# A fused attention and feed-forward kernel: x and q's factors brought into channel order by transposing transfers

## The chip, the cores and the metric

The kernel runs on one core of one Trainium2 chip. The metric is the device time of one launch in microseconds, as the median of three runs. A core has a matrix engine (TensorE, PE), a vector engine (VectorE, DVE), an activation engine (ScalarE, ACT), a general engine (GpSimd, POOL) and a queue engine (SyncE, SP) that here issues transfers; each goes through its own list of instructions in order, and they wait for each other through semaphores. 16 DMA engines do the transfers. SBUF is the on-chip memory of 128 partitions, PSUM the memory that TensorE writes.

## The reference, cut to what matters

```python
xn = layernorm(x)                                  # x: 2 x 2048 tokens x 256 channels
# attention on xn: a second layernorm with gain and bias, then
z = layernorm(xn) * g + b
q, _, v = split(z @ w_in.T + b_in); k = q          # 16 heads of 16 channels
out = softmax(q @ k.T / 4) @ v ; attn = out @ w_out.T + b_out
# feed-forward on xn, with weights rounded to -1, 0, 1
h = gelu(xn @ ternary(W1).T + b1); ffn = h @ ternary(W2).T + b2
return x + attn + ffn
```

The second normalisation of an already normalised token is one number per token, the factor. So q = (the product of xn with the scaled weights) times the factor of the token, plus a bias.

## The kernel before, in words

The 4096 tokens go through the first stage in 8 groups of 512 (NG = 8), each as 4 tiles of 128 tokens. After it comes the attention over 32 pairs of batch and head, paced by VectorE's row maxima (line 889), and the output projection. The change touches only the first stage, some 200 of 1397 us.

TensorE contracts over partitions, so it needs x with channels on partitions ("channel order"), while the normalisation makes it with tokens on partitions ("token order"). Before, this goes as follows in group g:

- VectorE in `stats_of(g + 1)` and `norm(g + 1)`: means and variances of the next group (L754 to L764), a power on GpSimd (`rsqrt`, L657), then `xn` in token order (L772) and the factor columns (L777). GpSimd spreads the factor over 128 columns (`replicate`, L662).
- TensorE at the start of its `group(g)`: 8 transpositions of `xn` (L1170) and 4 of the factor replicas (L1154), all float32 128x128, into the PSUM banks `tr_x` and `tr_f`.
- ScalarE copies `tr_x` scaled to float16 (`x1`, L1038) and `tr_f` to `factor_rows` (L1031). VectorE makes the remainder, `x2 = tr_x * 256 - x1` (`second_parts`, L784). x1 + x2 carries x nearly in float32 precision through float16 products.
- TensorE then: the second half of the values of group g - 1 (`values(g-1, 1)`, L1135), the down projection of g - 1 (`ffn_down`, L1115, 64 products), the q products of g (L1135, 12), the up projection (L1198, 8 columns of weights f = 0 to 7, two PSUM banks in turn, so that f waits for the GELU of f - 2), with the first half of the values after f = 3.
- From group 2 on, TensorE puts steps of the first head's row maxima between (`between`, L359, 4 in a group), which VectorE reduces (`first_rows`, L889).
- VectorE in a group: `second_parts(g)`, `stats_of(g+1)`, `value(g-1, 1)` (L802), `norm(g+1)`, `add_ffn(g-1)` twice (L810), `q_split(g)` (L791 twice, L795 twice), and `results(g)`: 4 remainders of the hidden layer (L881) with row maxima between. ScalarE: the first part of q (L1059) as soon as L791 has made it, then GELU twice (L1063) and the first part of the hidden layer (L1068), four times.
- SyncE: `store_q(g)` (L545, 2 transfers). After group 1 and after group 3 it waits for the stores and loads pieces of the first heads (8, then 24 transfers, L553 to L556), in the same queue.

The order is written out by hand in each engine's program. In the attention SyncE uses one small transposing transfer in each head (L564, 128x128 float16).

## Time and profile before

| | us |
|---|---|
| median of 3 runs (lowest, highest) | 1397.49 (1397.26, 1397.63) |
| the profiled execution: its own time | 1398.74 |
| its span, first to last instruction | 1397.0 |
| TensorE busy | 1367.5 (98%) |
| VectorE busy | 1328.5 (95%) |
| ScalarE busy | 1236.8 (89%) |
| GpSimd busy | 141.4 (10%) |

The mean granted TensorE clock is 0.994 of full speed. The shares are means over stages with different limits: what a change of the first stage is worth is read from that stage.

### The profile page before, as it was taken

Reading aid. Unit: us, or ns where it says so; the run is one execution under the profiler, and the core shown is the slowest. Engines: PE = TensorE matmul, PEld = TensorE weight load, DVE = VectorE, ACT = ScalarE, POOL = GpSimd, SP = SyncE. Lnnn points to the kernel's source line nnn. Section 1 sums busy time; section 2 is a strip of 40 time slices with the busy share of each in tenths; the row PEclk is TensorE's granted clock in tenths of the full one; section 3 lists DMA queues with packets and bytes.
Section 4 is the critical chain, followed back from the end, with each engine's and each line's share of the span. In section 5 each row is a group of like instructions: output and inputs, shape, how many; then the busy total and the mean of one; then the engine's idle time right before and its main releaser. Section 6 shows DMA issues by size and latency. Waiting matters only on the chain.

```text
span 1397.0 us, 32162 instructions
## 1 busy us (share of the span) xinstructions
PE 1367.5 (98%) x13350; PEld 467.5 (33%) x13350; DVE 1328.5 (95%) x1396; ACT 1236.8 (89%) x2244; POOL 141.4 (10%) x351
## 2 busy tenths in 40 slices
PE   6999999999999999999999999999999999999999
PEld 4656643222222222222222222222222222222244
DVE  6898999999999999999999999999999999999935
ACT  5564638999999999999999999899999999999975
POOL 2101034000000000000000000000222200002200
PEclk8999999999999999999999999999999999999999
DMA  6112000011110001001001001001122201012122
GB/s 239 27 38 65 31 18 2 33 32 33 33 33 33 32 33 33 33 33 33 33 33 33 32 31 35 26 28 39 51 64 60 63 32 34 33 35 63 40 89 98
DMA packets 33916, 61.75 MB, mean 44 GB/s; under 512 B 11392, under 2 KB 16928, under 8 KB 33514
## 3 DMA queue, kind: packets, MB, share of 16 engines
q1 hardware_dynamic: 33194, 58.04, 12.5%
q8 instruction: 105, 1.72, 0.5%
q10 hardware_dynamic: 576, 1.65, 0.3%
q14 instruction: 41, 0.34, 0.1%
HBM read 41.29 MB, written 16.77 MB: 42 GB/s over the span
## 4 chain that ended last, share of the span: by engine, by line
DVE 70%; PE 25%; issue 2%; DMA 1%; ACT 1%; POOL 0%; ACTq 0%; SPq 0%; DVEq 0%; POOLq 0%
DVE part_max L889 68%; PE ps L389 6%; PE ps L403 3%; PE ps L1198 3%; PE ps L359 3%; PE ps L1115 3%; PE ps L1135 2%; PE ps L480 2%; PE ps L461 1%; DMA rows<-in_rows 1%; ACT w L1092 1%; PE ps L450 1%; PE ps L490 0%; PE ps L1170 0%; DMA max_rows<-max_split 0%
## 5 line engine op out<-in xcount | busy, mean ns | idle before, releaser
L1092 ACT ACTIVATE w<-ps 128x512 f32<-128x512 f32 x2048 | 1109.5, 596 | 65.9 <-PE ps L403 16.5
L889 DVE TENSOR_REDUCE part_max<-ps 128x1 f32<-128x1024 f32 x1024 | 1161.1, 1212 | 4.1 <-PE ps L359 3.8
L389 PE MATMUL ps<-w,v_ones 128*32 128x256 f32 (+1 forms) x7688 | 627.8, 398 | 0.6 <-DVE resid L810 0.3
L403 PE MATMUL ps<-qry,key 50*128 50x512 f16 x1984 | 399.0, 387 | 7.7 <-ACT w L1092 6.9
L359 PE MATMUL ps<-qry,key 48*128 48x512 f16 x2048 | 393.9, 381 | 5.3 <-DVE part_max L889 5.3
L389 PEld LDWEIGHTS ps<-w,v_ones 128*32 128x32 f32 x7688 | 151.5, 108 | 313.2 <-issue 160.7
L403 PEld LDWEIGHTS ps<-qry,key 50*128 50x128 f16 x1984 | 98.1, 92 | 430.2 <-ACT w L1092 412.1
L359 PEld LDWEIGHTS ps<-qry,key 48*128 48x128 f16 x2048 | 99.9, 93 | 82.6 <-DVE part_max L889 16.6
L681 POOL COPY v_ones<-v_all 128x128 f32<-128x128 f32 x64 | 18.7, 293 | 748.8 <-PE ps L389 748.8
L1059 ACT ACTIVATE q_split<-q_by_factor,sigma_bq 128x512 f16<-128x512 f32 x16 | 11.1, 719 | 63.0 <-DVE q_by_factor L791 62.6
L1198 PE MATMUL ps<-x,w_ternary 128*128 128x512 f16 x256 | 62.4, 382 | 1.6 <-ACT hidden L1063 1.6
L1115 PE MATMUL ps<-w_ternary,w 128*128 128x256 f16 x448 | 51.3, 273 | 0.2 <-DVE w L881 0.2
L1063 ACT ACTIVATE hidden<-ps,columns 128x512 f32<-128x512 f32 x64 | 41.8, 678 | 6.6 <-PE ps L1198 5.6
L1115 PEld LDWEIGHTS ps<-w_ternary,w 128*128 128x128 f16 x448 | 43.3, 98 | 6.7 <-issue 1.4
L955 DVE SCALAR_TENSOR_TENSOR resid<-ps,y_unscale,resid 128x512 f32<-128x512 f32 x16 | 12.0, 750 | 33.1 <-PE ps L480 33.1
L881 DVE SCALAR_TENSOR_TENSOR w<-hidden,hidden_scale,w 128x1024 f16<-128x1024 f32 x28 | 35.7, 1281 | 6.5 <-ACT w L1068 6.5
L688 POOL TENSOR_TENSOR max_rise<-part_max 128x16 f32<-128x16 f32 x32 | 7.9, 248 | 274.4 <-DVE part_max L889 274.4
L1198 PEld LDWEIGHTS ps<-x,w_ternary 128*128 128x128 f16 x256 | 22.6, 98 | 32.9 <-issue 6.8
L1068 ACT ACTIVATE w<-hidden,hidden_scale 128x1024 f16<-128x1024 f32 x28 | 32.2, 1149 | 1.0
L1135 PE MATMUL ps<-x,wq_parts 128*128 128x512 f16 x96 | 24.6, 410 | 3.7 <-ACT factor_rows L1031 3.7
L657 POOL TENSOR_TENSOR rstd<-var_eps,minus_half 128x8 f32<-128x8 f32 x8 | 13.5, 1690 | 118.5 <-DVE var_eps L764 118.5
L1135 PE MATMUL ps<-wv_parts,x 128*128 128x256 f16 x192 | 23.6, 273 | 0.0
(151 smaller groups left out, 481.1 us busy)
## 6 DMA issues: line engine op xcount, KB each, us to landing
key<-q_parts SPq DMA_DIRECT2D x62, 128.0 KB
qry<-q_parts SPq DMA_DIRECT2D x62, 128.0 KB
o_heads<-o_evacuated SPq DMA_DIRECT2D x31, 256.0 KB, 9.8
key<-q_parts SPq DMA_DIRECT2D x66, 64.0 KB
qry<-q_parts SPq DMA_DIRECT2D x66, 64.0 KB
resid<-in_x SPq DMA_DIRECT2D x8, 512.0 KB, 13.7
q_parts<-q_split SPq DMA_DIRECT2D x16, 256.0 KB, 2.3
out<-resid SPq DMA_DIRECT2D x7, 512.0 KB, 4.7
```

Of the source, the lines that this page charges most:

```text
L359: mm = eng.matmul(pair[:, j * BANK:(j + 1) * BANK], key[v][r:r + ROWS, blk * P:(blk + 1) * P], qry[v][r:r + ROWS, c * BANK:(c + 1) * BANK] ...
L389: mm = eng.matmul(pv[32 * c:32 * c + 2 * D, c0:c1], vst[:, kb, :], prob[kb % 2][:, c * BANK + c0:c * BANK + c1], start=(kb == 0), stop=(kb ...
L403: eng.matmul(ring_bank(v, i, False), key[v][r:r + KROWS, kb * P:(kb + 1) * P], qry[v][r:r + KROWS, c * BANK:(c + 1) * BANK], start=True, s ...
L480: mm = eng.matmul(py[:, j * C:(j + 1) * C], o_parts(g, k)[0:rows, a, t * P:(t + 1) * P], wop[0:rows, b, k, :], start=(m == 0), stop=(m == ...
L881: dve.scalar_tensor_tensor(out=part[1], in0=hid[:, 2 * i:2 * i + 2, :], scalar=hs[:, 0:1], in1=part[0], op0=ALU.mult, op1=ALU.subtract).th ...
L889: dve.tensor_reduce(part_max[h % 2][:, blk, side:side + 1], pa[a % 2], AX.X, ALU.max).then_inc(s_r, 1)
L1063: act.activation(hid[:, f, :], pf[f % 2], ACT.Gelu, scale=1.0 / XS, bias=b1_col[:, f:f + 1]).then_inc(s_g, 1)
L1068: act.activation(parts_of(g)[0][:, f - 1:f + 1, :], hid[:, f - 1:f + 1, :], ACT.Identity, scale=hs[:, 0:1]).then_inc(s_h1, 1)
L1092: act.activation(prob[kb % 2][:, c * BANK:(c + 1) * BANK], ring_bank(k, i, last), ACT.Exp, scale=exp_scale).then_inc(s_e, 1)
L1115: mm = pe.matmul(pf[t // 2][:, (t % 2) * C:(t % 2 + 1) * C], parts_of(g)[i][:, f, t * P:(t + 1) * P], w2t[:, f, :], start=(f == 0 and i == ...
L1135: mm = pe.matmul(out, rows(k, i, j), cols(k, i, j), start=(m == 0), stop=(m == len(terms) - 1))
L1198: mm = pe.matmul(pf[f % 2], w1t[:, k, f * P:(f + 1) * P], part[:, k, :], start=(k == 0 and i == 0), stop=(k == KC - 1 and i == 1))
```

## The change

For groups 1 to 7 the float16 parts of x are made in token order and both are transposed by one transfer; the same for the factors, split into two float16 parts by GpSimd. Group 0 stays on TensorE. The float32 factor is scaled by 2^14 before it is split, and the products with `factor_rows` take 2^-14 back.

- ScalarE: `stage_first(g+1)` makes 256 * `xn` in float16, 128x1024, in place of L1038 twice and L1031. It stands ahead of q's first part.
- VectorE: `stage_second(g+1)` makes the remainder, 128x1024, and stands between `add_ffn` and `q_split`; `second_parts` ahead of `stats_of` goes.
- GpSimd: `replicate` makes two float16 parts of the replicas (a small scaling, a cast, a subtraction of 128x512); `factor_rows(g)` adds the two transposed parts (128x512).
- SyncE: `x_parts_in(g+1)` ahead of `store_q(g)`: a transfer of 8 blocks of 128x128 for the factors and one of 16 blocks for x.
- TensorE: from group 1 on no transpositions; q waits for `s_xt`, the x transfer.

```diff
+        xt = [sb(f"x_parts{i}", [P, 2, KC, BANK], F16) for i in range(2)]
+        xs = scr[:, 2:4, :].rearrange("p i n -> p (i n)").bitcast(F16).rearrange("p (s n) -> p s n", s=2)
...
+            def x_parts_in(g):
+                sp.wait_ge(s_fb, 3 * g + 1)
+                wait(sp, s_fr, g)
+                sp.dma_start_transpose(f_parts[:, :, :].rearrange("p s (t n) -> p (s t) n", n=P),
+                                       f_rep_parts[:, :, :, :].rearrange("p s t n -> p (s t n)")).then_inc(s_fx, 16)
+                sp.wait_ge(s_xs, g)
+                wait(sp, s_v, 2 * (g - 1))
+                sp.dma_start_transpose(xt[g % 2][:, :, :, :].rearrange("p s k (t n) -> p (s k t) n", n=P),
+                                       xs[:, :, :].rearrange("p s n -> p (s n)")).then_inc(s_xt, 16)
...
-            for g in range(HALF_GROUPS):
+            def group(g):
+                if g + 1 < NG:
+                    x_parts_in(g + 1)
                 store_q(g)
...
             def replicate(g):
                 pool.wait_ge(s_fc, 2 * (g + 1))
-                wait(pool, s_ft, g)
-                pool.tensor_copy(f_rep[:, :, :], f_col[:, g % 2, :].unsqueeze(2).to_broadcast((P, TG, P))).then_inc(s_fp, 1)
+                pool.tensor_tensor(f_big[:, :], f_col[:, g % 2, :], f_times[:, :], ALU.mult).then_inc(s_fb, 1)
...
+                pool.tensor_copy(f_rep_parts[:, 0, :, :], big).then_inc(s_fb, 1)
+                pool.wait_ge(s_fb, 3 * g)
+                pool.tensor_tensor(f_rep_parts[:, 1, :, :], big, f_rep_parts[:, 0, :, :], ALU.subtract).then_inc(s_fb, 1)
+
+            def factor_rows(g):
+                pool.wait_ge(s_fx, 16 * g)
+                pool.wait_ge(s_qf, KC * g)
+                pool.tensor_tensor(f_row[:, :], f_parts[:, 0, :], f_parts[:, 1, :], ALU.add).then_inc(s_fr, 1)
...
+            def stage_second(g):
+                dve.wait_ge(s_xa, g)
+                wait(dve, s_xt, 16 * (g - 1))
+                dve.scalar_tensor_tensor(out=xs[:, 1, :], in0=xn[:, :, :].rearrange("p a b -> p (a b)"), scalar=XS, in1=xs[:, 0, :],
+                                         op0=ALU.mult, op1=ALU.subtract).then_inc(s_xs, 1)
...
             for g in range(1, NG - 1):
-                second_parts(g)
+                if g == 1:
+                    stage_second(1)
                 stats_of(g + 1)
...
                     add_ffn(g - 1, j)
+                stage_second(g + 1)
                 q_split(g)
...
+            def stage_first(g):
+                act.wait_ge(s_ln, 4 * g + 4)
+                wait(act, s_xt, 16 * (g - 1))
+                act.activation(xs[:, 0, :], xn[:, :, :].rearrange("p a b -> p (a b)"), ACT.Copy, scale=XS).then_inc(s_xa, 1)
...
                 wait(pe, s_vd, 2 * g)
-                pe.wait_ge(s_x2, KC * (g + 1))
-                pe.wait_ge(s_fr, g + 1)
+                if first:
+                    pe.wait_ge(s_x2, KC)
+                    pe.wait_ge(s_fr, 1)
+                else:
+                    pe.wait_ge(s_xt, 16 * g)
```

How the change moves instructions, at three places. First VectorE from the last hidden remainder of one group to the q products of the next, before:

```order
L881 SCALAR_TENSOR_TENSOR w<-hidden,hidden_scale,w 128x1024
L784 SCALAR_TENSOR_TENSOR x<-ps,x 128x512 x2
L754 BN_STATS stats<-resid 128x6 x4
L757 MEMSET wait_carrier 128x1
L759 BN_AGGR mean_var<-stats 128x2 x4
L763 TENSOR_SCALAR var_eps<-mean_var 128x4
L764 TENSOR_SCALAR var_eps<-mean_var 128x4
L802 SCALAR_TENSOR_TENSOR v_all<-ps,factor_columns,scaled_bv 128x256 x2
L770 TENSOR_TENSOR root_of_var<-var_eps,rstd 128x4
L772 TENSOR_SCALAR xn<-resid,mean_var,rstd 128x256 x4
L810 SCALAR_TENSOR_TENSOR resid<-ps,hidden_unscale,resid 128x512 x2
L791 TENSOR_TENSOR q_by_factor<-ps,factor_rows 128x512 x2
```

and now (`weight_scratch` is the tensor in which the staged parts `xs` lie):

```order
L936 SCALAR_TENSOR_TENSOR w<-hidden,hidden_scale,w 128x1024
L799 BN_STATS stats<-resid 128x6 x4
L804 BN_AGGR mean_var<-stats 128x2 x4
L808 TENSOR_SCALAR var_eps<-mean_var 128x4
L809 TENSOR_SCALAR var_eps<-mean_var 128x4
L857 SCALAR_TENSOR_TENSOR v_all<-ps,factor_columns,scaled_bv 128x256 x2
L815 TENSOR_TENSOR root_of_var<-var_eps,rstd 128x4
L817 TENSOR_SCALAR xn<-resid,mean_var,rstd 128x2x128 x4
L865 SCALAR_TENSOR_TENSOR resid<-ps,hidden_unscale,resid 128x512 x2
L838 SCALAR_TENSOR_TENSOR weight_scratch<-xn,weight_scratch 128x1024
L845 SCALAR_TENSOR_TENSOR q_by_factor<-ps,factor_rows 128x512 x2
```

The x remainder moved from the start of this stretch, for group g, to its end, for group g + 1, directly ahead of the q products.

TensorE at the boundary of two groups, before:

```order
L1198 MATMUL ps<-x,w_ternary 128x512 x8
L1170 MATMUL ps<-ident_f,xn 128x128 x8
L1154 MATMUL ps<-ident_f,factor_replicas 128x128 x4
L1135 MATMUL ps<-wv_parts,x 128x256 x12
L1115 MATMUL ps<-w_ternary,w 128x256 x64
L1135 MATMUL ps<-x,wq_parts 128x512 x12
```

and now:

```order
L1258 MATMUL ps<-x_parts,w_ternary 128x512 x8
L1196 MATMUL ps<-wv_parts,x_parts 128x256 x12
L1176 MATMUL ps<-w_ternary,w 128x256 x64
L1196 MATMUL ps<-x_parts,wq_parts 128x512 x12
```

The twelve transpositions are gone, and nothing else moved on TensorE.

SyncE's queue from the q store of group 0, before:

```order
L545 DMA q_parts<-q_split 128x2x512 x4
L553 DMA key<-q_parts 32x1x1024
L554 DMA key<-q_parts 16x1024
L555 DMA qry<-q_parts 32x1x1024
L556 DMA qry<-q_parts 16x1024
```

and now:

```order
L557 DMA q_parts<-q_split 128x2x512 x2
L563 DMA_TRANSPOSE factor_parts<-factor_replicas 128x8x128
L567 DMA_TRANSPOSE x_parts<-weight_scratch 128x16x128
L563 DMA_TRANSPOSE factor_parts<-factor_replicas 128x8x128
L567 DMA_TRANSPOSE x_parts<-weight_scratch 128x16x128
L557 DMA q_parts<-q_split 128x2x512 x2
L575 DMA key<-q_parts 32x1x1024
```

Two transposing transfers stand ahead of each q store and, through it, ahead of the loads of the first heads.

## Rows read from the trace of the kernel before

**Rows 1.** The page, part 4: the chain that ended last, by engine and by line.
```profile
DVE 70%; PE 25%; issue 2%; DMA 1%; ACT 1%; POOL 0%; ACTq 0%; SPq 0%; DVEq 0%; POOLq 0%
DVE part_max L889 68%; PE ps L389 6%; PE ps L403 3%; PE ps L1198 3%; PE ps L359 3%; PE ps L1115 3%; PE ps L1135 2%; PE ps L480 2%; PE ps L461 1%; DMA rows<-in_rows 1%; ACT w L1092 1%; PE ps L450 1%; PE ps L490 0%; PE ps L1170 0%; DMA max_rows<-max_split 0%
```

**Rows 2.** The chain in order of time, groups 2 and 3: start us, us, what.
```profile
73.33 0.32 PE ps L359 x2
...
82.39 0.87 PE ps L1170 x8
83.27 0.44 PE ps L1154 x4
...
97.07 1.83 PE ps L1198 x8
...
104.52 0.87 PE ps L1170 x8
```

**Rows 3.** Busy time in group 3: stretch, length, each engine (instructions), clock, DMA share, GB/s.
```profile
82.39:104.52 22.13, 22.13 (x155) 14.30 (x153) 20.00 (x38) 12.57 (x18) 2.25 (x2) 1.00 0.11 36
```

**Rows 4.** Timeline of group 3: start, us, engine, line, operation [idle before <-releaser].
```profile
84.51 1.28 DVE L881 SCALAR_TENSOR_TENSOR w<-hidden,hidden_scale,w 128x1024 f16<-128x1024 f32 x1 [0.26 <-ACT w L1068]
...
85.84 1.29 DVE L784 SCALAR_TENSOR_TENSOR x<-ps,x 128x512 f16<-128x512 f32 x2
...
89.22 1.64 POOL L657 TENSOR_TENSOR rstd<-var_eps,minus_half 128x8 f32<-128x8 f32 x1 [17.98 <-DVE var_eps L764]
90.95 0.16 DVE L770 TENSOR_TENSOR root_of_var<-var_eps,rstd 128x4 f32<-128x4 f32 x1 [1.04 <-POOL rstd L657]
...
92.40 1.40 DVE L810 SCALAR_TENSOR_TENSOR resid<-ps,hidden_unscale,resid 128x512 f32<-128x512 f32 x2
...
93.72 0.68 DVE L791 TENSOR_TENSOR q_by_factor<-ps,factor_rows 128x512 f32<-128x512 f32 x1
```

**Rows 5.** Timeline of group 1.
```profile
42.88 1.28 DVE L784 SCALAR_TENSOR_TENSOR x<-ps,x 128x512 f16<-128x512 f32 x2
43.02 4.26 PEld L1115 LDWEIGHTS ps<-w_ternary,w 128*128 128x128 f16 x40 [0.45 <-DVE w L881]
...
47.40 2.75 PE L1135 MATMUL ps<-x,wq_parts 128*128 128x512 f16 x12
...
50.76 1.27 DVE L791 TENSOR_TENSOR q_by_factor<-ps,factor_rows 128x512 f32<-128x512 f32 x2
...
53.51 1.90 PE L1198 MATMUL ps<-x,w_ternary 128*128 128x512 f16 x8 [1.38 <-ACT hidden L1063]
...
60.67 0.41 SPq L556 DMA_DIRECT2D qry<-q_parts  x1
```

**Rows 6.** Timeline of group 7, the first row maxima.
```profile
177.82 4.62 DVE L889 TENSOR_REDUCE part_max<-ps 128x1 f32<-128x1024 f32 x4 [1.40 <-PE ps L359]
```

**Rows 7.** The small transposing transfer, line 564: issue min/median/max in ns, then landing.
```profile
L564 SPq DMA_TRANSPOSE max_rows<-max_split x32: 1119/1132/1216, 202.3 to 1331.8; - x32
...
DMA to landing us min/median/max: 2.2/2.2/4.3
```

**Rows 8.** What the DMA engines moved, 40 slices of 203.0 to 204.4 us.
```profile
GB/s 0 0 0 0 0 0 0 0 0 0 0 0 0 0 0 73 95 183 219 190 117 51 7 0 234 0 0 0 0 0 0 0 0 1 0 1 1 0 0 0
```

**Rows 9.** The page, part 5: ScalarE's 128x1024 copies (busy us, mean ns | idle).
```profile
L1068 ACT ACTIVATE w<-hidden,hidden_scale 128x1024 f16<-128x1024 f32 x28 | 32.2, 1149 | 1.0
```

**Rows 10.** GpSimd's nearest operations: min/median/max ns, first and last start.
```profile
L714 POOL TENSOR_TENSOR x<-below_half,x x2: 1158/1160/1161, 1276.2 to 1279.3; 128x512 f16<-128x512 f32 x2
...
L688 POOL TENSOR_TENSOR max_rise<-part_max x32: 217/217/1183, 198.8 to 1330.3; 128x16 f32<-128x16 f32 x32
```

**Rows 11.** Granted clock around TensorE's idle time in group 0 (columns as in rows 3).
```profile
13.00:14.00 1.00, 0.34 (x4) 0.10 (x1) 0.00 (x0) 0.00 (x0) 0.00 (x0) 1.00 1.01 383
...
15.00:16.00 1.00, 0.00 (x0) 0.00 (x0) 0.56 (x2) 1.00 (x3) 0.37 (x1) 0.50 1.00 410
...
28.50:29.00 0.50, 0.50 (x4) 0.26 (x3) 0.49 (x1) 0.50 (x1) 0.50 (x1) 0.99 0.00 0
```

More of the change, by code:

```diff
@@ L32 @@
 HTOP = 2.0 ** 14
+FS = 2.0 ** 14
 AHEAD = 2
@@ L205, in attention_ffn @@
         r_rest = [f32(t, n)[0:HR, :] for t in (w1t, w2t) for n in range(2)]
-        on = [hid[:, n, :].bitcast(F16).rearrange("p (s n) -> p s n", s=2) for n in range(NT0)] + [x1, x2] + on_k
+        on = [hid[:, n, :].bitcast(F16).rearrange("p (s n) -> p s n", s=2) for n in range(NT0)] + [xt[0][:, s, :, :] for s in range(2)] + on_k
         on_rest = [scr[0:HR, n, :].bitcast(F16).rearrange("p (s n) -> p s n", s=2) for n in range(NCH)]
@@ L265, in attention_ffn @@
         s_x2 = sem("x2")
+        s_xa = sem("x_part1_staged")
+        s_xs = sem("x_part2_staged")
+        s_xt = sem("x_parts_transposed")
         s_fc = sem("factor_columns")
@@ L574, in _ @@
             sp.wait_ge(s_pad, 16 * (2 * ROT - 1))
-            for g in range(HALF_GROUPS):
+            def group(g):
+                if g + 1 < NG:
+                    x_parts_in(g + 1)
                 store_q(g)
+            store_q(0)
+            x_parts_in(1)
+            for g in range(1, HALF_GROUPS):
+                group(g)
             sp.wait_ge(s_qs, 16 * KC * HALF_GROUPS)
@@ L579, in _ @@
             for g in range(HALF_GROUPS, NG // NB):
-                store_q(g)
+                group(g)
             sp.wait_ge(s_qs, 16 * KC * NG // NB)
@@ L585, in _ @@
             for g in range(NG // NB, NG):
-                store_q(g)
+                group(g)
             sp.wait_ge(s_qs, 16 * KC * NG)
@@ L767, in norm @@
                 x = resid[:, g * TG:(g + 1) * TG, :]
-                wait(dve, s_tr, g)
+                wait(dve, s_tr, min(g, 1))
                 dve.wait_ge(s_rs, g + 1)
@@ L1071, in _ @@
             group(0, True)
+            act.wait_ge(s_wvp, 1)
+            stage_first(1)
             for g in range(1, NG):
@@ L1136, in part_products, with parts_x @@
                 return mm
-            xp = (x1, x2)
+            def parts_x(g):
+                return [xt[g % 2][:, i, :, :] for i in range(2)]
             def values(g, j):
@@ L1150, in factor_transposes @@
             def factor_transposes(g):
-                pe.wait_ge(s_fp, g + 1)
-                wait(pe, s_fr, g)
+                pe.wait_ge(s_fp, 1)
                 for t in range(TG):
@@ L1155, in factor_transposes @@
                 mm.then_inc(s_ft, 1)
-            def step_count(g):
-                return len(BETWEEN) * (min(max(0, g - HALF_GROUPS), HALF_GROUPS) + max(0, g - NG // NB))
             def group(g, between=None, between_down=None):
-                pe.wait_ge(s_ln, 4 * g + 4)
-                wait(pe, s_x2, KC * g)
-                if g == 1:
+                first = g == 0
+                xp = parts_x(g)
+                if first:
+                    pe.wait_ge(s_ln, 4)
+                    for k in range(KC):
+                        for t in range(TG):
+                            mm = pe.transpose(tr_x[k][:, t * P:(t + 1) * P], xn_kt[:, k, t, :], idf[:, :])
+                    mm.then_inc(s_tr, 1)
+                    abs_total(0)
+                    factor_transposes(0)
+                if g == HALF_GROUPS:
                     pe.wait_ge(s_wd, 5)
                     pe.wait_ge(s_od, 1)
-                wait(pe, s_r, step_count(g))
-                for k in range(KC):
-                    for t in range(TG):
-                        mm = pe.transpose(tr_x[k][:, t * P:(t + 1) * P], xn[:, t, k * P:(k + 1) * P], idf[:, :])
-                mm.then_inc(s_tr, 1)
-                first = g == 0
-                if first:
-                    abs_total(0)
-                factor_transposes(g)
                 if first:
@@ L1182, in group @@
                 wait(pe, s_vd, 2 * g)
-                pe.wait_ge(s_x2, KC * (g + 1))
-                pe.wait_ge(s_fr, g + 1)
+                if first:
+                    pe.wait_ge(s_x2, KC)
+                    pe.wait_ge(s_fr, 1)
+                else:
+                    pe.wait_ge(s_xt, 16 * g)
                 for o in range(KC):
```

67 lines of the change are left out of this document (40 added, 27 removed).

## The prediction

> **What bounds the kernel now.** I read the chain of waits first. Over the whole kernel it is VectorE with 70%, nearly all of it row maxima [rows 1]: from about 178 us on the kernel runs at VectorE's pace, and what reaches that point earlier ends earlier by as much. Before that point the same chain in order of time lies on TensorE: in group 3 it enters the transpositions of x at 82.39 and those of the factors at 83.27, leaves them at 83.70 (83.27 + 0.44), and is back at the same place at 104.52 [rows 2]. A group takes 22.13 us, of which 1.31 are transpositions. The busy time by stretch shows what stands close behind: VectorE is busy for 20.00 of these 22.13 us [rows 3], and 1.04 of the rest is its wait for GpSimd's power at 90.95 [rows 4], which no edit touches. So VectorE needs 21.04 us a group as it stands, TensorE without transpositions 22.13 - 1.31 = 20.82. TensorE cannot get all of its 1.31 us; the question is where VectorE and ScalarE stop it.
>
> **The loop that is left in groups 2 to 6.** The x remainder costs VectorE the same in either place: 1.29 us for its two PSUM halves [rows 4], and 1.28 for one 128x1024 from SBUF, by the hidden remainder of that form [rows 4]. The scaled q products are of the form of L784, which takes 0.68 like L791, so they cost nothing more. But the remainder moves from the start of VectorE's stretch, where TensorE had time, to directly ahead of the q products. Follow one turn:
>
> - from TensorE's last up product to the end of the last hidden remainder: 82.39 to 84.51 + 1.28 = 85.79, 3.40 us through two GELUs and a copy on ScalarE. Unchanged, as it hangs on TensorE's end.
> - from there to the start of the q products: 93.72 - 85.79 = 7.93 us, with L784 in it before, with the staged remainder after. VectorE is busy or waits for GpSimd's power throughout, so these 7.93 stay. ScalarE's part fits: L810 starts at 92.40, so xn is done by then, the copy takes 1.15 [rows 9], the two L810 take 1.32 to the next row.
> - from the q products' start to TensorE's f = 2, which needs the first GELU, which stands behind q's first part on ScalarE: 2.75 us, as group 1 shows, where TensorE waited for it: 50.76 to 53.51 [rows 5].
> - from f = 2 to the group's end on TensorE: 104.52 - 97.07 = 7.45 us [rows 2].
>
> Sum: 3.40 + 7.93 + 2.75 + 7.45 = 21.53 us a turn, against TensorE's own 20.82. Before, TensorE needed 22.13 and this loop had 0.6 us to spare; now the loop decides, and TensorE waits 0.71 us ahead of f = 2. **A group gains 22.13 - 21.53 = 0.6 us, not 1.31.** Five groups (2 to 6): -3.0 us.
>
> **Group 7.** VectorE sits idle for 1.40 us until TensorE's first step at 177.8 [rows 6]. The step stands behind the transpositions, so here all 1.31 us are gained; with the end of the idle time VectorE's row maxima begin, and the gain is carried to the end. -1.31 us.
>
> **Group 1.** Its transpositions cover nothing: TensorE waited right after them for VectorE's last hidden remainder until 43.02, with 40 down products left [rows 5]. So the q products can again start at 47.40 at the earliest, and now they need the x transfer. VectorE ends the staged remainder where L784 ended, at 42.88 + 1.28 = 44.16, and SyncE, with the factors' transfer long behind it, issues 16 blocks. The trace has a transfer of one block only: 1.13 us of issue and 2.2 to landing [rows 7], its data in 8 slices of 35 ns, 0.28 us, at 219 GB/s at the most [rows 8]. That leaves about 0.8 us after the data. Bounds for 16 blocks (512 KB): at 219 GB/s 1.1 + 2.4 + 0.8 = 4.3 us; with the 0.28 of a block 16 times 1.1 + 4.5 + 0.8 = 6.4; with the whole issue time of a block 16 times 18 + 1.1 = 19 us. I take 6.0, near the second, as the one block's data came in one burst and not spread over its issue. x then lands at 50.2. ScalarE may write the parts of group 2 only then: 1.15 us, VectorE 1.28, and the q products start at 52.7 instead of 50.76 [rows 5] (up to 5.4 us it would be 52.04, since the remainder follows L810 anyway). TensorE's f = 2 follows 2.75 us later, as before: +1.9 us.
>
> The Trainium skill prices such a transfer in two ways. "Advanced Engine Details and Errata", section X-Bar Transpose (TRN2), expects 350 to 400 GB/s, by which the data would take an estimated 1.4 us and the landing stay under 5.4 us; its rate isn't seen in the one block of this trace, 219 at the peak. "VectorE: DVE Perf Modes", section The three transpose paths, gives 1309 ns for a 128x128 block, near the issue of 1.13 here; if that holds for every block of a large transfer, the second rival below is what happens.
>
> **What else is added, and what hides it.** GpSimd makes the parts and adds them up, three operations of up to 1.16 us [rows 10] and a small one, about 3 us in a group in which it was busy for 2.25 [rows 3]; the rows are needed a group later. SyncE's 24 blocks stand ahead of the q store: at 0.28 a block plus two fixed costs some 9 of 21.5 us. The store lands later by as much, which ScalarE asks for only in the next group, and the loads of the first head after it (8 behind group 1, 24 behind group 3), whose first use is a step of the following group, had 12 us: the last of the 8 was issued by 61.1 [rows 5], the first step ran at 73.33 [rows 2]. The 24 behind group 3 take, at 0.41 or somewhat more each, 10 to 14 us and end about when the factors' parts of group 5 are ready. Nothing on the chain at that price. Losing this cover starts when SyncE's work exceeds a group.
>
> **Sum.** +1.9 - 3.0 - 1.31 = -2.4 us: 1396.3 against the profiled execution's 1398.74, and 1397.49 - 2.4 = **1395.1** against the median of the runs, which lies 1.25 below that execution. Its own range, from the bounds of the landing (4.3 gives +1.3, about 8 gives +3.9) and 0.3 us either way in each of five turns: 1393 to 1398.5.
>
> **Rivals.**
> 1. TensorE stays the bound, the loop closes faster than I add up. For it: TensorE is busy in all of the 22.13 us, and VectorE has 2.13 spare by the sum of its busy time. Against it: the order of the four links. It would give -6 x 1.31 + 1.3 = -6.6, 1390.9. Chance 0.12.
> 2. Transposing transfers cost per block. For it: the issue of one block takes 1.13 us, where that of a plain load of the first head takes 0.41 [rows 5]. Against it: the short burst [rows 8]. It turns the sign from where the x transfer lands 8.4 us after its issue (2.4 more than 6.0), so from 0.4 us a block. At 0.6 a block the landing takes 11.5 us and the sum is +3, 1400.6, with SyncE at 15 of 21.5 us and the 24 loads ahead of group 5's parts about to add some; at 1.13 a block SyncE alone needs 28 us a group, q of group 7 starts some 60 us late, and the time is near 1460. Chance 0.20, most of it in the lower half.
> 3. GpSimd's new work slows VectorE, with which it runs side by side: the subtraction falls on the staged remainder, which reads two SBUF tensors. For it: GpSimd's L688 took 1183 ns once instead of 217 [rows 10], so something can hold it up. Against it: no row here shows VectorE held up. If 1.16 us are lost in the loop in five groups, -2.4 + 5.8 = +3.4, 1400.9; from 0.5 us a group it is slower. Chance 0.08.
> 4. TensorE's clock falls in group 1. In group 0 TensorE went idle at 13.34, and the granted clock was 0.50 (1.2 GHz) by 15; it was back at 2.4 GHz from 28.5, 6 us after TensorE had resumed [rows 11]. The new wait ahead of q is 50.2 - 47.4 = 2.8 us; an idle time of 1.38 in this group brought no fall [rows 5]. Six us of products at half speed lose 3 us, partly beside the q products' own wait: +2, so 1397.1, within no change. Chance 0.15.
>
> **How the numbers follow.** The forecast has 0.45. A measurement of this kernel tells no change from 0.2%, 2.8 us either way: 1394.7 to 1400.3. The forecast lies within it by 0.4 us, so a third of its chance goes to faster (0.15), with rival 1 (0.12) that makes 0.27. Slower are rival 2 except its mild third (0.14), rival 3 in half its sizes (0.05) and 0.05 for rivals 3 and 4 or 2 and 4 together: 0.24. The rest, 0.49, is no change. The range reaches to 1390 for rival 1 and to 1403 for the mild half of rivals 2 and 3.
>
> **What would show it.** In the profile after: TensorE idle for some 0.7 us ahead of an up projection (f = 2) in groups 2 to 6, released by a GELU, and turns of 21.5 us; q products of VectorE right behind the staged remainder; TensorE idle for 2 to 3 us ahead of q in group 1, released by the x transfer; that transfer's landing near 6 us and SyncE's issue of it near 5; the first row maxima of group 7 near 175.4. Turns of 20.8 speak for rival 1; an issue of x near 10 or 18 us for rival 2; VectorE's 128x1024 remainder longer than 1.28 for rival 3; a clock of 0.5 near 50 us for rival 4. The forecast is wrong if the turns are under 21.2 or over 21.9, or if group 1 costs over 4 us.

## The result, and the profile after

| | before | after |
|---|---|---|
| median, us (lowest, highest; runs) | 1397.64 (1397.26, 1397.99; 6) | 1403.70 (1402.01, 1407.72; 6) |
| ratio to before, 95% interval | | 1.0044 (1.0035 to 1.0054) |
| profiled execution, its span | 1398.74, 1397.0 | 1403.02, 1401.2 |

Slower by 6.1 us, where 2.4 less were forecast, and outside the range (1403.0). The two profiled executions, from which all rows below are, lie 4.3 us apart: that of the kernel before is 1.1 us above its median, that of the kernel after 0.7 below. First the busy time of one turn, the stretch from one start of VectorE's q products to the next, which answers to [rows 3]. Columns: the stretch, its length, busy time of PE, PEld, DVE, ACT, POOL with their instructions, PE's granted clock, DMA share, GB/s.

```profile
97.34:119.47 22.13, 20.88 (x142) 12.97 (x140) 20.27 (x37) 11.82 (x15) 5.19 (x5) 1.00 0.47 111
```

TensorE's work did shrink to 20.88 us, and the turn is still 22.13, as before. VectorE's way to the q products, in order of time (start, duration, engine, line), answers to [rows 4]:

```profile
92.73 0.17 DVE L815 TENSOR_TENSOR root_of_var<-var_eps,rstd 128x4 f32<-128x4 f32 x1 [1.06 <-POOL rstd L685]
94.18 1.40 DVE L865 SCALAR_TENSOR_TENSOR resid<-ps,hidden_unscale,resid 128x512 f32<-128x512 f32 x2
95.50 1.92 DVE L838 SCALAR_TENSOR_TENSOR weight_scratch<-xn,weight_scratch 128x1024 f16<-128x1024 f32 x1
97.34 1.27 DVE L845 SCALAR_TENSOR_TENSOR q_by_factor<-ps,factor_rows 128x512 f32<-128x512 f32 x2
```

GpSimd at the same time:

```profile
94.61 0.61 POOL L699 CAST factor_replicas<-factor_scaled 128x512 f16<-128x512 f32 x1
95.30 1.04 POOL L701 TENSOR_TENSOR factor_replicas<-factor_scaled,factor_replicas 128x512 f16<-128x512 f32 x1
```

And all seven staged remainders (minimum, median, maximum in ns):

```profile
L838 DVE SCALAR_TENSOR_TENSOR weight_scratch<-xn,weight_scratch x7: 1211/1918/1922, 43.9 to 164.3; 128x1024 f16<-128x1024 f32 x7
```

The remainder that was priced at 1.28 takes 1.92 wherever GpSimd's subtraction had begun 0.20 us before it, and 1.21 the one time (43.9) that GpSimd was idle. TensorE waits behind it for the GELU, for 1.42 us at 77.97 and 1.25 at 168.94.

TensorE in group 1, answering to [rows 5], and the two transfers:

```profile
43.99 4.54 PE L1176 MATMUL ps<-w_ternary,w 128*128 128x256 f16 x40 [0.93 <-DVE w L936]
49.50 2.75 PE L1196 MATMUL ps<-x_parts,wq_parts 128*128 128x512 f16 x12 [0.98 <-DMA x_parts<-weight_scratch]
56.27 1.90 PE L1258 MATMUL ps<-x_parts,w_ternary 128*128 128x512 f16 x8 [2.28 <-ACT hidden L1122]
```

```profile
L567 SPq DMA_TRANSPOSE x_parts<-weight_scratch x7: 1771/2026/4330, 45.1 to 166.5; - x7
DMA to landing us min/median/max: 4.3/4.4/8.0
L563 SPq DMA_TRANSPOSE factor_parts<-factor_replicas x7: 1232/1239/9487, 34.1 to 165.2; - x7
DMA to landing us min/median/max: 3.2/3.3/14.2
```

f = 2 comes at 56.27 instead of 53.51: +2.8 us, although x lands sooner than was taken, 4.4 us after its issue. The maxima (4330 ns of issue, 9487 ns, 14.2 us) are one place, SyncE's queue behind group 3:

```profile
103.50 0.63 SPq L575 DMA_DIRECT2D key<-q_parts  x1
...
117.63 2.37 SPq L577 DMA_DIRECT2D qry<-q_parts  x1
120.05 2.14 SPq L578 DMA_DIRECT2D qry<-q_parts  x1
122.30 9.49 SPq L563 DMA_TRANSPOSE factor_parts<-factor_replicas  x1
131.88 4.33 SPq L567 DMA_TRANSPOSE x_parts<-weight_scratch  x1
```

and what hangs on it, on GpSimd and then on VectorE:

```profile
136.59 1.15 POOL L706 TENSOR_TENSOR factor_rows<-factor_parts 128x512 f32<-128x512 f16 x1 [18.12 <-DMA factor_parts<-factor_replicas]
137.70 1.65 POOL L685 TENSOR_TENSOR rstd<-var_eps,minus_half 128x8 f32<-128x8 f32 x1
```

```profile
139.45 0.16 DVE L815 TENSOR_TENSOR root_of_var<-var_eps,rstd 128x4 f32<-128x4 f32 x1 [3.51 <-POOL rstd L685]
```

GpSimd adds the rows of group 5 before it makes the power of group 6, in program order; the rows' parts land at 136.5, so VectorE's wait for the power is 3.51 us instead of 1.06. In group 7 TensorE's first products for row maxima begin at 181.63; the first row maximum, which answers to [rows 6], is at 182.07 instead of 177.82, +4.2 us, and that difference stays to the end (span 1401.2 against 1397.0).

### The profile page after: what moved, and what is told of

It reads as the page before. It is cut to its first block, busy times and chain, and to the rows that moved or that the text cites. A ratio compares the mean times of both kernels' runs of the same rounds, so it can differ in the third digit from the quotient of the medians.

```text
span 1401.2 us, 32007 instructions
## 1 busy us (share of the span) xinstructions
PE 1357.5 (97%) x13266; PEld 456.4 (33%) x13266; DVE 1333.4 (95%) x1389; ACT 1232.2 (88%) x2230; POOL 161.5 (12%) x374
## 4 chain that ended last, share of the span: by engine, by line
DVE 79%; PE 12%; DMA 3%; ACT 2%; issue 2%; SPq 1%; POOL 1%; ACTq 0%; DVEq 0%
DVE part_max L944 73%; PE ps L401 3%; PE ps L492 2%; PE ps L415 2%; PE ps L1258 1%; PE ps L371 1%; PE ps L473 1%; DMA factor_parts<-factor_replicas 1%; DMA rows<-in_rows 1%; DVE weight_scratch L838 1%; DVE w L936 1%; ACT hidden L1122 1%; PE ps L462 1%; DMA max_rows<-max_split 1%; POOL rstd L685 1%
## 5 line engine op out<-in xcount | busy, mean ns | idle before, releaser
L1258 PE MATMUL ps<-x_parts,w_ternary 128*128 128x512 f16 x256 | 61.9, 380 | 10.1 <-ACT hidden L1122 10.1
L1091 ACT ACTIVATE weight_scratch<-xn 128x1024 f16<-128x1024 f32 x7 | 7.4, 1054 | 45.0 <-DVE xn L817 45.0
L1258 PEld LDWEIGHTS ps<-x_parts,w_ternary 128*128 128x128 f16 x256 | 22.4, 98 | 41.0 <-ACT hidden L1122 14.2
L1196 PE MATMUL ps<-x_parts,wq_parts 128*128 128x512 f16 x96 | 23.5, 397 | 6.6 <-ACT factor_rows L1086 3.7
L1196 PE MATMUL ps<-wv_parts,x_parts 128*128 128x256 f16 x192 | 23.6, 273 | 0.0
```

The costliest lines, as they stand in the source:

```text
L1196: mm = pe.matmul(out, rows(k, i, j), cols(k, i, j), start=(m == 0), stop=(m == len(terms) - 1))
L1258: mm = pe.matmul(pf[f % 2], w1t[:, k, f * P:(f + 1) * P], part[:, k, :], start=(k == 0 and i == 0), stop=(k == KC - 1 and i == 1))
```

## The experiments

All are told by one ruler: the start of VectorE's q products in groups 1 to 7 (L791 before, L845 after), from the trace of each. Turns are the differences. Each ratio is to the kernel before in the same session (its medians there were 1397.6 to 1398.2), so ratios compare better than medians.

| kernel | starts, us | turns | median, ratio (95%) |
|---|---|---|---|
| before | 50.8 71.8 93.7 115.9 138.0 160.1 185.9 | 21.0 21.9 22.1 22.1 22.1 25.8 | |
| after | 53.5 75.2 97.3 119.5 144.1 166.2 190.2 | 21.7 22.1 22.1 **24.6** 22.1 24.0 | 1403.70, 1.0044 |
| e1_spread | 53.8 77.1 99.2 121.3 143.5 165.6 189.6 | 23.3 22.1 22.1 22.1 22.1 24.0 | 1402.07, 1.0028 (1.0017 to 1.0040) |
| e2_onepart | 52.1 73.1 94.5 115.9 139.4 162.1 186.1 | 21.0 21.4 21.4 23.6 22.7 24.0 | 1399.08, 1.0004 (0.9995 to 1.0013) |
| e3_order | 52.3 72.1 93.0 113.8 142.9 164.3 188.8 | 19.9 20.9 20.9 **29.1** 21.4 24.5 | 1400.65, 1.0023 (1.0014 to 1.0032) |
| e4_xonly | 51.4 72.3 93.8 115.2 138.2 159.8 184.3 | 21.0 21.4 21.4 23.0 21.6 24.4 | 1396.89, 0.9990 (0.9981 to 0.9999) |
| e5_order_spread | 51.9 71.7 92.6 113.5 134.3 155.2 179.5 | 19.9 20.9 20.9 20.9 20.9 24.3 | 1392.32, 0.9962 (0.9949 to 0.9976) |
| e6_xonly_order_spread | 49.7 69.7 91.4 113.3 135.3 157.2 183.1 | 19.9 21.7 21.9 21.9 21.9 25.9 | 1396.23, 0.9987 (0.9978 to 0.9996) |
| e9_late_subtraction | 52.8 73.8 95.2 116.6 144.8 166.2 190.2 | 21.0 21.4 21.4 **28.2** 21.4 24.0 | 1402.88, 1.0042 (1.0028 to 1.0055) |
| e10_start | 50.3 70.1 91.0 111.9 132.8 153.6 177.9 | 19.9 20.9 20.9 20.9 20.9 24.3 | 1390.94, 0.9954 (0.9941 to 0.9968) |
| e11_late_spread | 53.0 74.0 95.5 116.9 138.3 159.7 183.7 | 21.0 21.4 21.4 21.4 21.4 24.0 | 1396.91, 0.9993 (0.9984 to 1.0002) |
| e12_late_spread_start | 51.2 72.2 93.6 115.0 136.4 157.9 181.9 | 21.0 21.4 21.4 21.4 21.4 24.0 | 1395.42, 0.9983 (0.9974 to 0.9992) |

**e1_spread: the queue alone.**

```diff
             load_columns(0, 0, L // 2, L // 2, s_ld[0])
-            for h in range(1, ROT):
-                load_head(h, h)
             for g in range(NG // NB, NG):
                 group(g)
+                if g - NG // NB + 1 < ROT:
+                    load_head(g - NG // NB + 1, g - NG // NB + 1)
```

> The 16 loads of heads 1 and 2 are issued 8 by 8 behind groups 4 and 5 instead of all behind group 3, so the transfers of the parts of group 5 no longer stand behind 24 loads. Queue theory: the factors' transfer of group 5 lands in 3 to 5 us instead of 14.2, VectorE's wait for GpSimd's power in group 5 falls from 3.51 to 1.06 us, 2.5 us less in all (near 1401), and the runs lie closer together. Rival (GpSimd against VectorE explains all of the loss): no change beyond 0.5 us.

The long turn is gone (22.12), the staged remainder still takes 1.92. The profiled execution lost 1.6 us of its gain in an earlier turn (23.3 for 21.7): TensorE waited 2.30 us ahead of f = 2 in group 1, and its products behind that, and a stretch within them, read

```profile
56.52 3.54 PE L1258 MATMUL ps<-x_parts,w_ternary 128*128 128x512 f16 x8 [2.30 <-ACT hidden L1122]
...
57.00:59.00 2.00, 2.00 (x6) 0.68 (x5) 0.74 (x1) 1.74 (x3) 0.82 (x1) 0.50 1.09 298
```

a granted clock of 0.50 (1.2 GHz) where the kernel after has 1.00 (2.4 GHz) with an idle time of 2.28 at the same place, and 1.90 us for the same 8 products. That is what the fourth rival described. In the trace the gain of the turn is plain, 2.5 us; in the times it is 1.6 us, smaller than expected, with an interval that overlaps that of the kernel after. The seven executions do lie closer together, as expected: 1401.4 to 1402.8, against 1402.0 to 1407.7.

**e2_onepart: GpSimd's two-input operations out.** The second part of the factors is set to zero and the rows are a copy of the first: the factors have float16 precision only.

```diff
-                pool.tensor_tensor(f_rep_parts[:, 1, :, :], big, f_rep_parts[:, 0, :, :], ALU.subtract).then_inc(s_fb, 1)
+                pool.memset(f_rep_parts[:, 1, :, :], 0.0).then_inc(s_fb, 1)
...
-                pool.tensor_tensor(f_row[:, :], f_parts[:, 0, :], f_parts[:, 1, :], ALU.add).then_inc(s_fr, 1)
+                pool.tensor_copy(f_row[:, :], f_parts[:, 0, :]).then_inc(s_fr, 1)
```

> Leaves out the second float16 part of the factors of groups 1 to 7: GpSimd fills it with zeros instead of subtracting, and copies the first part instead of adding two. The transfers stay. Contention theory (VectorE's operations on two SBUF tensors are held up while GpSimd runs one with two inputs): the staged remainder takes 1.21 us in all seven groups instead of 1.92 in six, the stretched remainders near 33 and 37 us go back to 2.35 and 1.28, and the time falls by 0.95 + 6 x 0.71 = 5.2 us, to about 1398.5. Rival (the remainder is slow by its own form or because of the transfers): it stays at 1.92 and the time within 1 us.

```profile
L838 DVE SCALAR_TENSOR_TENSOR weight_scratch<-xn,weight_scratch x7: 1208/1215/1219, 43.1 to 161.0; 128x1024 f16<-128x1024 f32 x7
```

The remainder is back at 1.21 in all seven, although GpSimd's memset, which reads nothing, still lies beside its first 0.29 us (93.33 to 93.62), and two turns are 21.41 us: the forecast's loop of 21.53. The turn of 23.6 is the queue's. The one of 22.7 behind it begins with q products of TensorE at a granted clock of 0.50 (4.44 us for the 12 of 2.75), after 2.16 us of idle time, for which VectorE waits 0.97. The time fell by 4.6 us, near the expected 5.2.

**e3_order: the remainder behind the q products.** `q_split(g)` stands ahead of `stage_second(g + 1)`, nothing else changes.

> The staged remainder stands behind q_split instead of ahead of it. Loop theory (the place of the remainder ahead of the q products makes TensorE wait for the first GELU): TensorE's wait of 1.25 to 1.4 us at f = 2 goes, and a turn falls from 22.13 to what VectorE needs, 21.1 to 21.6: 5 x 0.5 to 1.0, time 1399 to 1401.5. The subtraction of GpSimd now falls on operations that read PSUM, so the remainder may take 1.21 as well. Rival (VectorE's sum of work decides, not the order): turns stay near 22.1, no change.

Turns of 20.87 us, TensorE's own time. But then one of 29.1: most of what was gained by group 4 is lost in the queue, whose end hardly moves (SyncE, factor parts and x parts of group 5; compare 122.30 and 131.88 in the kernel after):

```profile
121.60 9.34 SPq L563 DMA_TRANSPOSE factor_parts<-factor_replicas  x1
131.04 5.52 SPq L567 DMA_TRANSPOSE x_parts<-weight_scratch  x1
```

The loads begin at 102.82, where they began at 103.50, although group 3 is 4.4 us ahead: the x transfer of group 4 now waits for a later remainder (97.18), and the q store and the loads stand behind it. The long wait has a second price. TensorE is idle for 6.16 us, and then runs at a granted clock of 0.50 (1.2 GHz):

```profile
138.88 5.28 PE L1196 MATMUL ps<-x_parts,wq_parts 128*128 128x512 f16 x12 [6.16 <-DMA x_parts<-weight_scratch]
```

5.28 us for the 12 products that take 2.75 at 2.4 GHz.

**e4_xonly: the factors stay with TensorE, ScalarE and a GpSimd copy,** as in the kernel before; only x goes by transfer.

> Only x goes by transposing transfer; the factors go back to TensorE, ScalarE and the one copy on GpSimd, as in the kernel before. TensorE gets 0.44 us a group back. Contention theory: no two-input operation of GpSimd is left beside VectorE, the remainder takes 1.21 everywhere, the start gets 0.95 back and groups 1 to 6 0.71 each: -5.2; and the factors no longer wait behind the 24 loads, but the x parts of group 5 still do, where TensorE may wait 1 to 3 us: 1397 to 1399. Rival (the x transfer and the order alone make the loss): no better than 1402.

No operation of VectorE is lengthened that was not so in the kernel before, turns of 21.41, one of 23.0 behind the loads. The time is a shade under before (0.9981 to 0.9999) and 0.1 us under the expected range; the gain is in the turns.

**e5_order_spread and e6_xonly_order_spread: the edits together.** e5 is e3 and e1 in one; e6 is e4 with both.

> The changed kernel with both edits that helped alone: the staged remainder behind the q products (1400.65 alone) and the 16 loads of the second and third heads spread behind groups 4 and 5 (1402.07 alone). Theory (VectorE's turn held up by 0.7 us, and once the parts of group 5 late behind the loads): the two add up. The turns were 20.87 us wherever the queue did not interfere, and the one turn of 29.06 falls to about 20.9, so the last group starts some 8 us earlier than with the order alone; but of it VectorE's own work between 180 and 190 us keeps at least 2 to 3, as its row maxima then decide (TensorE waits 2.2 us for them there). 1392 to 1394, every turn 20.8 to 21.1. Rival (the loads are harmful through their transfers' bandwidth and not through their place in SyncE's queue): spread over two groups they slow two turns instead of one, about 1396 to 1398.

> Only x by transposing transfers, the factors transposed on TensorE and copied by ScalarE as before, with the staged remainder behind the q products and the loads spread. Nothing is added on GpSimd, so nothing lengthens VectorE's operations at the start (0.95 us in the changed kernel at 37 us), while TensorE keeps 0.43 us of factor transpositions in a group. Theory: turns 21.25 to 21.35 us, TensorE the bound, six turns cost 2.4 to 2.7 us against the kernel with both by transfer, the undisturbed start gives back 0.95: about 1.5 us slower than that one, 1393.5 to 1395.5. Rival (the head loads cost through bandwidth): 1396 to 1398, one or two turns of 23 us or more behind group 3.

e5 came out as the theory said: every turn from group 2 to group 6 20.87, and no wait of TensorE between 70 and 165 us; so the loads harm by their place in the queue. e6 missed its range by 0.7: its turns are 21.9, not 21.3. The four transpositions of the factors cost TensorE 0.6 us and, ahead of them, there is a wait of 0.45 to 0.49 us, in the trace for VectorE's row maxima, for which the program makes the transpositions wait; I had priced only the first.

**e7_before_two and e8_before_one: the contention by itself.** The kernel before, with one GpSimd operation more in a group on data that nothing uses. One execution of each was taken (1398.94 and 1403.80 us), for its rows and not for its time.

```diff
+                pool.wait_ge(s_h1, KF // 2 * (g - 1) + 2)
+                wait(pool, s_pr, g)
+                pool.tensor_tensor(probe_out[:, :], probe_in[:, :], probe_in[:, :], ALU.subtract).then_inc(s_pr, 1)
```

> The kernel before with one GpSimd operation more in a group, on data that nothing uses: a subtraction of 128x512 with two float32 inputs from SBUF, float16 out, begun when VectorE begins its second hidden remainder (L881, 128x1024, two SBUF inputs, 1.28 us). Theory (a two-input operation on GpSimd holds up a VectorE operation that reads two SBUF tensors while it lasts): the remainder beside it takes 1.9 to 2.3 us, seven of 40 in the whole kernel, the others stay at 1.28. Rival (the staged remainder was slow in the changed kernel by something of its own, its target in the scratch tensor or the same replicas' writes): all stay at 1.28 us. The time is of no interest here: between no change and +4 us.

> As the run with the added subtraction, but with a copy on GpSimd in its place: one float32 input (128x512, read four times), float16 out, 128x2048, begun at the same moment. Theory (it takes two SBUF inputs on both engines): the hidden remainder beside it stays at 1.27 to 1.29 us, as the cast of 128x512 in the changed kernel lengthened nothing. Rival (any GpSimd work on SBUF holds up VectorE's two-input operations): 1.7 us or more beside it.

With the subtraction, GpSimd and VectorE at 57 us (the hidden remainder is L889 here, 1.28 alone):

```profile
57.10 1.04 POOL L678 TENSOR_TENSOR probe_out<-probe_in 128x512 f16<-128x512 f32 x1 [7.44 <-ACT w L1076]
...
57.05 2.17 DVE L889 SCALAR_TENSOR_TENSOR w<-hidden,hidden_scale,w 128x1024 f16<-128x1024 f32 x1 [1.05 <-ACT w L1076]
```

With the copy of one input:

```profile
57.51 1.89 POOL L678 CAST probe_out<-probe_in 128x2048 f16<-128x2048 f32 x1 [7.42 <-ACT w L1076]
...
57.48 3.00 DVE L889 SCALAR_TENSOR_TENSOR w<-hidden,hidden_scale,w 128x1024 f16<-128x1024 f32 x1 [1.05 <-ACT w L1076]
...
101.92 1.89 POOL L678 CAST probe_out<-probe_in 128x2048 f16<-128x2048 f32 x1 [7.89 <-ACT w L1076]
...
102.59 2.30 DVE L889 SCALAR_TENSOR_TENSOR w<-hidden,hidden_scale,w 128x1024 f16<-128x1024 f32 x1
```

Here my theory fell and its rival held: one input on GpSimd does the same. The remainder is longer by nearly the time that both are on: 1.04 us together cost 0.89, 1.89 cost 1.72, 1.22 (102.59 to 103.81) cost 1.02, and 0.84 (95.50 to 96.34 in the kernel after) cost 0.71. So it stands still until GpSimd has done; in the two rows at 57 us the records let VectorE begin 0.05 and 0.03 us ahead, too little to say who was first. In the other direction, where VectorE had begun 0.7 us earlier, GpSimd stands still: the first subtraction of e7, beside a float32 operation with two inputs that ran from 33.30 to 35.65, takes 2.51 us instead of 1.04.

```profile
34.04 2.51 POOL L678 TENSOR_TENSOR probe_out<-probe_in 128x512 f16<-128x512 f32 x1 [1.86 <-ACT w L1076]
```

The Trainium skill, "SBUF — State Buffer", section Who interferes with whom, states this as an exclusive lock on a port pair that the two share: whichever starts first has it for the whole instruction, when VectorE reads two SBUF tensors and GpSimd reads SBUF. The rows here agree, but for those two at 57 us, which are too close to decide the order.

Two SBUF inputs are not the only case. VectorE's L742, 128x2048 with a single SBUF tensor as input, runs once alone and once beside 0.32 us of GpSimd's copy of the factors (32.10 to 32.71) in the kernel before, and beside the whole 0.61 us of the cast (31.48 to 32.09) in the kernel after, where it is L787:

```profile
21.52 1.29 DVE L742 TENSOR_SCALAR below_half<-w,nhalf 128x2048 f32<-128x2048 f32 x1
32.39 1.40 DVE L742 TENSOR_SCALAR below_half<-w,nhalf 128x2048 f32<-128x2048 f32 x1
31.48 1.69 DVE L787 TENSOR_SCALAR below_half<-w,nhalf 128x2048 f32<-128x2048 f32 x1
```

0.32 us together cost 0.11 and 0.61 cost 0.40, again the common time less 0.2.

**e9_late_subtraction: the contention taken out, nothing left out.**

```diff
                 pool.wait_ge(s_fb, 3 * g)
+                if g > 1:
+                    pool.wait_ge(s_xs, g)
                 pool.tensor_tensor(f_rep_parts[:, 1, :, :], big, f_rep_parts[:, 0, :, :], ALU.subtract).then_inc(s_fb, 1)
```

> The changed kernel, in which from group 2 on GpSimd begins its subtraction (L701) only when VectorE has made the staged remainder (L838). Nothing is left out and VectorE's order is the changed kernel's. The run with the added copy showed that VectorE's operation with two SBUF inputs stands still while GpSimd's runs, whatever GpSimd reads (1.23 us side by side cost 1.02), and that row maxima and other operations that read PSUM lose nothing. Theory (one of the two engines at a time for such operations, VectorE with PSUM apart): the remainder takes 1.21 us instead of 1.92, the subtraction now lies beside the q products, which read PSUM and one SBUF tensor and keep their 0.68 us each; turns 22.13 - 0.71 = 21.4 us, five of them -3.5 us, so 1400.2 (1399.5 to 1401), a little more if GpSimd's later addition of the rows (L706) falls on a hidden remainder. Rival (the remainder is slow by its own place): still 1.9 us, the time stays at 1403 to 1404.

The mechanism is as expected and the time is not. GpSimd's subtraction now runs beside the q products, which read PSUM and one SBUF tensor and lose nothing:

```profile
94.06 1.22 DVE L840 SCALAR_TENSOR_TENSOR weight_scratch<-xn,weight_scratch 128x1024 f16<-128x1024 f32 x1
95.19 1.28 DVE L847 SCALAR_TENSOR_TENSOR q_by_factor<-ps,factor_rows 128x512 f32<-128x512 f32 x2
...
95.42 1.04 POOL L703 TENSOR_TENSOR factor_replicas<-factor_scaled,factor_replicas 128x512 f16<-128x512 f32 x1 [1.65 <-DVE weight_scratch L840]
```

Turns of 21.43; then one of 28.2, which ends at 144.8, where the kernel after had 144.1. I had forgotten what e3 shows: what is gained ahead of group 4 waits there for the queue, whose loads begin at 103.60 here. By its interval the time can't be told from that of the kernel after. One contention is left, here and in e11 and e12: GpSimd's addition (L706 after, L708 here) now reaches the first hidden remainder, which takes 1.60 to 1.69 us instead of 1.28. It is off the path: e2, where no remainder in the loop is lengthened, has the same turns of 21.41.

**e10_start: the start of e5.** Group 1's subtraction waits for the second ternary weights, its addition for the staged remainder.

```diff
+                if g == 1:
+                    pool.wait_ge(s_wd, 8)
                 pool.tensor_tensor(f_rep_parts[:, 1, :, :], big, f_rep_parts[:, 0, :, :], ALU.subtract).then_inc(s_fb, 1)
...
+                if g == 1:
+                    pool.wait_ge(s_xs, 1)
                 pool.tensor_tensor(f_row[:, :], f_parts[:, 0, :], f_parts[:, 1, :], ALU.add).then_inc(s_fr, 1)
```

> The kernel with the staged remainder behind the q products and the loads spread (1392.32), and in group 1 two GpSimd operations moved: the subtraction (L701, at 32.3 us) begins when the second ternary weights are done (L789), the addition of the rows (L706, at 37.5 us) when the staged remainder is (L838). Theory (VectorE's two-input operations stand still for them): L789 takes 2.35 instead of 3.01 us and the first hidden remainder 1.28 instead of 2.2, so VectorE's remainder of x in group 1 ends 1.6 us earlier, the x transfer lands at 48.1 instead of 49.7, and the turns of 20.87 behind it keep that: 1390.7 (1390 to 1391.5). Rival (the start hangs on the up products and GELU, and VectorE's lost time there is hidden): less than 0.5 us, 1392.

VectorE's ternary weights and first three hidden remainders (3.01 and 4.63 us without the edit, in e5):

```profile
33.38 2.35 DVE L793 SCALAR_TENSOR_TENSOR w_ternary<-w,half,below_half 128x2048 f16<-128x2048 f32 x1
36.86 3.68 DVE L940 SCALAR_TENSOR_TENSOR w<-hidden,hidden_scale,w 128x1024 f16<-128x1024 f32 x3
```

0.66 + 0.95 = 1.6 us, and 1.5 of it is kept in the span (1389.0 for 1390.5). This is the best version: 6.7 us under the kernel before, by the medians of its session.

**e11_late_spread and e12_late_spread_start: the changed kernel's own order, with both costs taken off its path.** e11 is e9 with e1's queue, e12 has e10's start as well.

> The changed kernel with its own order of VectorE's work, GpSimd's subtraction begun behind the staged remainder from group 2 on (L701 behind L838), and the loads of the second and third heads spread behind groups 4 and 5. Late subtraction alone gave turns of 21.43 us, as the forecast's four links say (21.53), but the turn behind group 3 then took 28.2 us, since the parts of group 5 came behind the loads at the same time as before: what was gained ahead of that point was lost there. Theory (the forecast's sum is right once the two costs that it left out are gone): turns of 21.0 and then 21.43 four times, q of group 7 at 52.8 + 21.0 + 4 x 21.43 + 24.0 = 183.5 us, a span of 1394.5 (1211 us behind that point, as in the changed kernel), the time near 1396.3. Rival (spread loads slow the turns they fall in): one or two turns over 22.5 us, 1398 or more.

> As the last, and in group 1 the subtraction begins behind the second ternary weights (L789) and the addition of the rows (L706) behind the staged remainder: the three places of contention and the queue are gone, the changed kernel's order is kept. Theory: the start 1.6 us earlier as in the run with those two moved (1392.32 to 1390.94), so 1394.7, which is the forecast of 1395.1 with the x transfer landing 4.4 us after its issue instead of 6.0. Rival (with VectorE's turns as the limit the start is hidden, unlike where TensorE's were): 1396.

The four turns from group 2 to group 6 are 21.41 to 21.43 in both; 1396.91 and 1395.42. One turn of e11, to be read against that of the kernel after: VectorE is busy for 19.81 us instead of 20.27, and TensorE has the same work in 0.71 us less.

```profile
95.45:116.87 21.42, 20.88 (x141) 12.97 (x140) 19.81 (x38) 11.82 (x15) 4.66 (x5) 1.00 0.36 80
```

## Why the prediction was wrong

**The loop was right, its gain a little too high.** 3.40 + 7.93 + 2.75 + 7.45 = 21.53 us was forecast; without contention and queue it is 21.42 (e9, e11, e12), and TensorE waits 0.54 us ahead of f = 2, 0.72 in group 2. The first rival would need 20.8, which only another order reaches (e3, e5). But the forecast took 0.6 us off five turns of 22.13, and the first two of them had been 21.0 and 21.9 in the kernel before: in e12 the five gain 0.0, 0.5 and three times 0.7, 2.7 us where 3.0 were added up.

**The x transfer was sized too high, harmlessly.** 4.4 us to landing, next to the lower bound of 4.3, where I took 6.0; 2.0 us of issue where I took about 5. The second rival is out: 16 blocks issue in 2.0 us, 8 in 1.24, one in 1.13 [rows 7]. Group 1 would have cost 51.2 - 50.8 = 0.4 us (e12) instead of 1.9, and the last turn gained 1.8 instead of 1.31.

**The step that failed first: GpSimd's three operations, "the rows are needed a group later".** I asked only who waits for their result, not what runs beside them. The third rival named the place and got 0.08 with "no row here shows VectorE held up". In groups 2 to 6 there is no such row, because no GpSimd operation of the kernel before lies there beside an operation of VectorE with two SBUF inputs; but an operation of VectorE with one SBUF input was held up at the start of that trace, L742 at 32.39 with 1.40 us instead of 1.29, and it was overlooked. The one of 1183 ns instead of 217 [rows 10] was GpSimd being held up in the same way (it began 0.16 us behind a hidden remainder of VectorE, at 198.75), and I noted it without drawing the other half. Measured: 0.71 us at each of six staged remainders, 4.3 us, and 1.6 at the start.

**The step that failed second: the 24 loads behind group 3, "nothing on the chain at that price".** I counted 10 to 14 us of issue, from the 0.41 of one load. They took 18.8 (103.5 to 122.3), the last two 2.4 and 2.1 us each. This price stood in the trace of the kernel before, whose same 24 loads take 18.4 us:

```profile
99.66 0.61 SPq L553 DMA_DIRECT2D key<-q_parts  x1
...
113.47 2.48 SPq L555 DMA_DIRECT2D qry<-q_parts  x1
115.99 2.11 SPq L556 DMA_DIRECT2D qry<-q_parts  x1
```

There nothing on the chain stood behind them. The transposition that now does took another 9.5 us to issue and 14.2 to land, and not only for its turn in the queue: the loads' data go on moving long after the last issue. In the kernel before, and then after (columns as in [rows 3]; the DMA share counts a packet's whole time where the packet begins, so it can exceed 1):

```profile
126.00:130.00 4.00, 4.00 (x36) 3.49 (x35) 3.56 (x5) 3.31 (x6) 0.00 (x0) 1.00 0.13 53
```

```profile
124.00:126.00 2.00, 2.00 (x17) 1.33 (x16) 2.00 (x3) 1.97 (x3) 0.00 (x0) 1.00 6.21 69
126.00:134.00 8.00, 8.00 (x59) 5.35 (x58) 7.63 (x10) 5.09 (x7) 0.00 (x0) 1.00 0.13 51
136.00:138.00 2.00, 2.00 (x19) 1.59 (x17) 0.00 (x0) 0.00 (x0) 1.41 (x2) 1.00 1.28 309
```

Packets that begin by 126 have a share of 6.21 and are thus under way for several us, then some 50 GB/s move until 134, the same rate as in the kernel before when only the loads' rest was moving, and the rate of 309 comes when that is over. That the transposition waits for this rest is the reading that fits; no run separates it from other causes within the queue.

It cost the turn 24.59 - 21.42 - 0.71 = 2.5 us, and 6.8 where the turns before it were as fast as forecast (e9: 28.2 - 21.4). Where this wall stands goes by when the loads begin, 103.5 in the kernel after and 102.8 and 103.6 in e3 and e9, so that group 5 starts at 144.1, 142.9 and 144.8 and most or all of what was gained ahead is taken back. In e2, whose q store is not delayed, they begin at 100.7, and group 5 starts at 139.4. That is why the parts don't add: contention alone in the loop -0.8 (e9, within the noise), queue alone -1.6 (e1), both -6.8 (e11), with the start -8.3 (e12), each median against 1403.70.

**The account.** From e12 to the kernel after, by the start of group 7's q products: 190.2 - 181.9 = 8.3 = 1.6 + 6 x 0.71 + 2.5. And e12 is at 0.9983 of before, -2.4 us, the forecast's number, and in part by chance. By the starts of group 7's q products e12 is 4.1 us ahead of the kernel before (181.9 for 185.9): +0.4 in group 1, -2.7 in the five turns, -1.8 in the last; by the spans 4.5 (1392.5 for 1397.0). The two profiled executions overstate it by 2.2 us, as that of the kernel before lies 1.1 above its median and that of e12 1.1 below.

What this account leaves open is the rest of the median's 6.1 us over the profiled executions' 4.3. TensorE's clock is a likely part: in the profiled executions of e2, e3 and e9, which keep the queue, the granted clock was 0.50 (1.2 GHz) for 3 to 7 us behind the long wait, between 137 and 145 us, and not in those of the kernel after, e1 and e11. Of the kernel after's six executions the four with the lowest mean granted clock (0.990 to 0.993) took 1403.7 to 1407.7 us, the two with 0.995 1402.0 and 1403.0. No trace of one of the four was kept, so this is not shown.

## What to carry to other kernels

Before work goes to GpSimd, list what VectorE runs beside it. In this kernel an operation of VectorE with two SBUF inputs stood still while GpSimd's copies and two-input operations ran, one with a single SBUF input lost time once too, and one that read PSUM did not, so the operation's time on GpSimd was a price on VectorE's path or nothing, by its place alone. A transfer that a stage waits for doesn't belong in a queue behind bulk loads; look in the trace before for how long those loads really take. And where one point in time is set by such a queue, an edit ahead of it reads as worthless until the queue is mended, so the two have to be tried together.
